# Two routed expert pairs in every unit of the shared expert, begun half a block later, and the last routed rows sent two to a product

## What is computed

```python
x = x + 0.5 * moe(layernorm(x))
x = x + mamba(layernorm(x))
x = x + 0.5 * moe(layernorm(x))

def moe(x):                              # 4096 tokens, 64 experts, 4 chosen for each token
    choice, weight = top4(x @ router_w.T + router_bias), softmax weights of those four, normed
    # each expert takes its first 64 tokens (capacity 64); the rest is dropped
    for e in experts:
        y[e] = (silu(x[tok[e]] @ gate_w[e].T) * (x[tok[e]] @ up_w[e].T)) @ down_w[e].T
        out[tok[e]] += y[e] * w[e]
    # the shared expert, hidden width 1024, sees every token
    return out + (silu(x @ sh_gate.T) * (x @ sh_up.T)) @ sh_down.T
```

## Time and profile before

| | us |
|---|---|
| median of 3 runs | 2441.6 (2437.28 to 2442.83) |
| profiled execution | 2441.09 |
| its span | 2439.3 |
| PE busy | 2349.8 (96% of the span) |
| DVE busy | 1415.3 (58%) |
| ACT busy | 956.4 (39%) |
| POOL busy | 665.4 (27%) |

### The profile page before, as it was taken

The page is one execution under the profiler, slowest core; times in us unless marked ns, Lnnn a source line. Parts: engine busy times, 40 slices in busy tenths (PEclk is TensorE's granted clock), DMA queues, the critical chain, the costliest instruction groups (busy, mean ns, idle before and its releaser), DMA issues.

```text
span 2439.3 us, 41942 instructions
## 1 busy us (share of the span) xinstructions
PE 2349.8 (96%) x16732; PEld 2073.8 (85%) x16732; DVE 1415.3 (58%) x3236; ACT 956.4 (39%) x1665; POOL 665.4 (27%) x524
## 2 busy tenths in 40 slices
PE   5999999999999999999999999998999999999995
PEld 5999997777788888888888889997999998787774
DVE  5777662222238777777777777776777762322221
ACT  4332332222236554445554555554333332323220
POOL 1244443111221222222222223220244443111121
PEclk9999999999998999999999999999999999999997
DMA  7644224877754110111111111013253314877758
GB/s 244 206 147 153 79 72 152 249 230 238 244 146 130 35 27 27 27 27 27 27 27 27 37 34 27 19 52 133 103 185 130 104 55 148 240 228 232 223 142 172
DMA packets 102754, 292.82 MB, mean 120 GB/s; under 512 B 22498, under 2 KB 22754, under 8 KB 91872
## 3 DMA queue, kind: packets, MB, share of 16 engines
q1 hardware_dynamic: 55216, 198.87, 23.3%
q0 software_dynamic: 47344, 91.27, 16.4%
HBM read 197.28 MB, written 151.80 MB: 143 GB/s over the span
## 4 chain that ended last, share of the span: by engine, by line
PE 93%; DVE 2%; DMA 1%; issue 1%; ACT 1%; another core or an unknown queue 0%; DVEq 0%; SPq 0%; POOLq 0%; ACTq 0%
PE m_p_ab L1559 5%; PE m_p_ab L1561 5%; PE m_p_ab L1560 5%; PE m_p_x L1559 3%; PE m_p_x L1561 3%; PE m_p_x L1560 3%; PE p_gate_b L688 3%; PE p_gate_a L688 3%; PE p_up_a L688 3%; PE p_up_b L688 3%; PE m_p_y L1660 3%; PE p_out_b L688 3%; PE p_gate_b L690 2%; PE p_gate_b L689 2%; PE p_x_a L786 2%; PE p_up_a L690 2%
## 5 line engine op out<-in xcount | busy, mean ns | idle before, releaser
L1852 DVE SCALAR_TENSOR_TENSOR m_xt<-m_ssm,m_convw,m_xt 128x256 f32<-128x256 f32 x384 | 218.9, 583 | 57.5 <-ACT m_ssm L1428 48.3
L1559 PE MATMUL m_p_ab<-m_ht_hi,m_wi_b_hi 128*128 128x256 f32 x640 | 182.4, 285 | 2.5 <-ACT m_gate L1400 2.5
L1561 PE MATMUL m_p_ab<-m_ht_hi,m_wi_b_lo 128*128 128x256 f32 x640 | 180.0, 281 | 0.0
L1560 PE MATMUL m_p_ab<-m_ht_lo,m_wi_b_hi 128*128 128x256 f32 x640 | 179.9, 281 | 0.0
L437 POOL DMA_INDIRECT slot_rows<-a_hr,a_slot_now x128 | 130.8, 1022 | 142.1 <-PE p_gate_a L690 85.7
L437 POOL DMA_INDIRECT slot_rows<-b_hr,b_slot_now x128 | 130.3, 1018 | 141.3 <-PE p_gate_b L690 85.6
L688 PE MATMUL p_gate_a<-a_hts_hi,a_w_hi 128*128 128x256 f32 x512 | 148.8, 291 | 7.3 <-DVE a_hts_lo L968 7.2
L688 PE MATMUL p_gate_b<-b_hts_hi,b_w_hi 128*128 128x256 f32 x512 | 148.4, 290 | 5.2 <-issue 5.1
L688 PE MATMUL p_up_a<-a_hts_hi,a_w_hi 128*128 128x256 f32 x512 | 148.9, 291 | 0.0
L688 PE MATMUL p_up_b<-b_hts_hi,b_w_hi 128*128 128x256 f32 x512 | 148.1, 289 | 0.0
L690 PE MATMUL p_gate_a<-a_hts_hi,a_w_lo 128*128 128x256 f32 x512 | 146.3, 286 | 0.0
(11 more groups left out here) (352 smaller groups left out, 7467.0 us busy)
## 6 DMA issues: line engine op xcount, KB each, us to landing
a_ew<-in_ew SPq DMA_DIRECT2D x32, 1536.0 KB, 7.2
b_ew<-in_ew SPq DMA_DIRECT2D x32, 1536.0 KB, 7.4
after_ffn<-a_zeros POOLq DMA_DIRECT2D x6, 2048.0 KB
out<-b_zeros POOLq DMA_DIRECT2D x6, 2048.0 KB
slot_rows<-a_zeros POOLq DMA_DIRECT2D x1, 8336.0 KB, 41.9
a_rows<-slot_rows SPq DMA_DIRECT2D x32, 260.5 KB, 8.5
b_rows<-slot_rows SPq DMA_DIRECT2D x32, 260.5 KB, 8.4
a_xr<-in_x SPq DMA_DIRECT2D x8, 1024.0 KB
```

Source lines behind the costliest of these rows:

```text
L1559: t.matmul(out, l_hi, r_hi_, start=first, stop=False)
L1560: t.matmul(out, l_hi, r_lo_, start=False, stop=False)
L1561: return t.matmul(out, l_lo, r_hi_, start=False, stop=last)
L1852: ins_ = v.scalar_tensor_tensor(xt[:, m, :], ssm[:, m, i:i + BM], convw[:, m, i:i + 1], xt[:, m, :], ALU.mult, ALU.add)
```

## The change

Three things change together. (1) Pairs no longer take two positions each but one and a half: gate and up of the even pair stand at p = 0 of a unit and those of the odd pair at p = 2. The first is at g = 117, the last down product at g = 165. The odd pair's `turn_prod` moves into the middle of the next unit's gate product. (2) The last 512 tokens' rows go out two to a product, over the second half of block 8 and the first half of block 9. (3) SP issues the first three pairs' loads in block 9 at g = 12*b + 6, and at that position a pair's loads now stand ahead of `load_xs`.

```diff
-PAIR_AT = (NR + 1) * POS + 3
+PAIR_UNIT = (NR + 1) * UN + 3
@@ positions of the pairs
         def begins(g):
-            q, odd = divmod(g - PAIR_AT, 2)
-            return q if not odd and 0 <= q <= PAIRS else None
-        def turns(g):
-            q, odd = divmod(g - PAIR_AT, 2)
-            return q if odd and 0 <= q < PAIRS else None
+            u, p = divmod(g, 3)
+            q = 2 * (u - PAIR_UNIT) + (p == 2)
+            return q if p != 1 and 0 <= q <= PAIRS else None
+        def turns_rows(g):
+            u, p = divmod(g, 3)
+            q = 2 * (u - PAIR_UNIT) + p
+            return q if p > 0 and 0 <= q < PAIRS else None
+        def turns_product(g):
+            u, p = divmod(g, 3)
+            q = 2 * (u - PAIR_UNIT) + (0 if p == 1 else -1)
+            return q if p < 2 and 0 <= q < PAIRS else None
@@ sync
-                        if g == b * POS + 6 and b + 2 < NS:
-                            load_xs(b + 2)
-                        if g == b * POS + POS - 1 and b == NR:
-                            for q in range(EU):
-                                load_pair(q)
                         q = begins(g)
                         if q and q - 1 + EU < PAIRS:
                             load_pair(q - 1 + EU)
+                        if g == b * POS + 6 and b + 2 < NS:
+                            load_xs(b + 2)
+                        if g == b * POS + 6 and b == NR + 1:
+                            for q in range(EU):
+                                load_pair(q)
@@ gpsimd
-                for b in range(NR + 1):
+                inv_std(1)
+                for b in range(1, NR + 2):
...
-                            if u >= UN // 2 and 1 <= b:
+                            if u >= UN // 2 and b <= NR:
                                 pool.wait_ge(full, b * UN + u + 1)
-                                some = 4 if b == NR else 2
-                                send_rows(b - 1, some * (n - UN), some)
+                                send_rows(b - 1, 2 * (n - UN), 2)
@@ tensor, gate_or_up, between the two halves m of a gate product
+                    if g == 0 and m == 1 and turns_product(3 * i) is not None:
+                        turn_prod(turns_product(3 * i))
@@ tensor, experts_at
-            if g == PAIR_AT - 1:
-                turn_rows(0)
                 q = begins(g)
                 if q is not None and q < PAIRS:
                     expert_gate_up(q)
                 if q:
                     expert_down(q - 1)
-                q = turns(g)
-                if q is not None:
-                    turn_prod(q)
-                    if q + 1 < PAIRS:
-                        turn_rows(q + 1)
+                q = turns_product(g)
+                if q is not None and g % 3:
+                    turn_prod(q)
+                q = turns_rows(g)
+                if q is not None:
+                    turn_rows(q)
```

More of the change, by code:

```diff
@@ L487, in program @@
                                 send_rows(b - 2, TR * K // 2 + 2 * n, 2)
-                            if u >= UN // 2 and 1 <= b:
+                            if u >= UN // 2 and b <= NR:
                                 pool.wait_ge(full, b * UN + u + 1)
-                                some = 4 if b == NR else 2
-                                send_rows(b - 1, some * (n - UN), some)
+                                send_rows(b - 1, 2 * (n - UN), 2)
                         if u == UN // 2 - 1 and b + 1 < NR:
                             inv_std(b + 1)
-                    if 1 <= b <= CLEARS:
+                    if b <= CLEARS:
                         clear_acc(b - 1)
@@ L612, in experts_at @@
             def experts_at(g):
-                if g == PAIR_AT - 1:
-                    rows_out(0)
                 q = begins(g)
@@ L619, in experts_at @@
                     expert_out(q - 1)
-                q = turns(g)
-                if q is not None and q + 1 < PAIRS:
-                    rows_out(q + 1)
+                q = turns_rows(g)
+                if q is not None:
+                    rows_out(q)
             def early(step):
@@ L1012, in experts_at @@
             def experts_at(g):
-                if g == PAIR_AT - 1:
+                if turns_rows(g) == 0:
                     dve.wait_ge(rows_loaded[0], 16)
@@ L1017, in experts_at @@
                     know(0)
+                q = turns_product(g)
+                if q is not None:
+                    product_turned(q)
                 q = begins(g)
@@ L1022, in experts_at @@
                         know(q + 1)
-                q = turns(g)
-                if q is not None:
-                    product_turned(q)
             def early(step):
```

## The result

The changed kernel takes 2399.79 us (median of 4 executions, 2398.56 to 2400.55) against 2440.17 us for the kernel before on the same chip (4, 2437.28 to 2442.83): a ratio of 0.9827, 95% interval 0.9812 to 0.9843. The forecast was 2432 with a range from 2411. The gain is 40 us in place of 9.6. The profiled execution spans 2397.7 us, 41.6 less than before's 2439.3.

The account below looks back on a forecast made before the run. PE was taken as bound, 96% busy, with losses at block 8's end, the chain of adds and the kernel's end. Layer a -6.6 and layer b -3.0 made 2441.1 - 9.6 = 2431.5, by the median 2432; range 2411 to 2461.

Parts of the forecast that it names:

- the chain: POOL's serial adds, one per pair and block; predicted to pace pairs from the fifth on and set layer b's end.
- s = 8.2: Assumed us per add, issue to issue, over the whole chain; between 5.69 without loads and 9.07 with a load beside each.
- 10.2 + 36 s - 308.4: Layer b's change: the chain starts 10.2 us later, takes 36 steps of s against 308.4 us now; forecast -3.0.
- Layer a, forecast -6.6: Layer a's sum: -8.2 for the removed wait after block 8, +1.6 for turns, 0 for PE waiting on adds.
- The stall: End of block 8: PE idle on a late semaphore, then slow clock; removal counted as -8.2 us layer a, -7.3 layer b.
- The 16 turns inside gate products, priced at +1.6: Turning the product inside the gate product adds 16 tile changes per layer, 0.1 us each: +1.6 in layer a, nothing in b.
- PE's wait for result buffers: Layer a's pairs: with five result buffers PE is free of the chain up to s = 8.3, so 0 us.
- Later start: Pairs begin six positions later, 17.5 us; PE loses nothing, but layer b's chain starts at +17.5 - 7.3 = +10.2.
- Order on SP: A pair's loads ahead of the token load cover one pair, 7.9 us, of a wait reaching 20 us; no gain counted.
- The merges begin about 10 us earlier: Kernel's end: merges start when the last pair is added, about 10 us earlier, with 51 us full DMA and 8 after.
- The rival with the nearest time, 2406: Adds become quick, s 7.0 or less, and PE bounds layer b's end: 2406 us, chance 0.12.
- the rival that they stay: The waits at the end of block 8 have another cause than the burst; 15.5 us come back: 2447 us, chance 0.13.

Follow-up runs that it names:

- Experiments 6: Kernel before, with every pair's weights load held back by one position, still evenly spaced: 2436.31 us, ratio 0.9984.
- experiment 7: Kernel before, with only every second pair's weights load held back by one position, so load distances alternate: 2425.07 us, ratio 0.9939.
- experiment 9: Kernel before, loading only the first half of each expert's packed weights from the fourth pair on: 2425.05 us, ratio 0.9936.
- experiment 8: Kernel before, with only SP's new order, a pair's loads ahead of the token load: 2440.4 us, ratio 1.0001.
- experiment 4: Changed kernel with the old order on SP, a block's token load ahead of the pair's loads: 2419.57 us, ratio 0.9928.
- experiments 2: Changed kernel without the new sends and later start (four to a product in block 8, pairs from unit 37): 2411.27 us, ratio 0.9889.
- 5: Changed kernel with the last 16 sends three to a product in block 8, two in block 9, pairs one unit earlier: 2395.37 us, ratio 0.9819.
- experiment 12: Version with last sends three to a product and pairs one unit earlier, run again beside the changed kernel: 2396.97 us, ratio 0.9817.
- experiment 3: Changed kernel with the last routed rows sent four to a product in block 8 again, all else as changed: 2421.89 us, ratio 0.9929.

## Why the prediction was wrong, step by step

**The step that failed is the time per step of the chain, s = 8.2,** in the term "10.2 + 36 s - 308.4" of layer b. It measured 7.43, and the 36 steps took 267.4 us in place of 295.2, 27.8 less. 7.43 lies between its bounds (5.69 and 9.07). The error has two parts.

The larger one needs no experiment. The prediction knew that a step without a load takes 5.69 us, but spread its 8.2, "nearer to the loaded end", over the whole chain. The last seven steps, from block 12's add to block 13's, have no weights load beside them and took 41.1 us where 8.2 gives 57.4: 16.3 of the 27.8 us. SP had asked for the last weights at 2287.13.

The rest is the loaded step: 212.3 us for 27 steps where 8.2 gives 221.4, 9.1 us, and 2.4 us in the first two. The prediction took it for a price of the add beside its load. Experiments 6, 7 and 9 showed in its place that the 9.07 of the kernel before was no such price: the chain had fallen in step with the loads, 9.15 us apart, and steps of 8.2 and 7.96 came out when only the loads' distances or bytes changed. In the changed kernel the stretch looked at had loads 7.65 us apart and steps of 7.67, and the mean from block 9 to 12, with the blocks' adds in it, is 7.86. How much of this its uneven distances do stays open. That loads would be asked for some 6.5 and 9.1 us apart was right (6.30 and 9.15).

**Layer a, forecast -6.6, measured -10.2** (the last finish 744.11, before 754.35). The stall is -8.1 of it (block 8's finish 391.57 against 400.70, less 1.0 that is there from the first block on and that the change does not explain). The 16 turns inside gate products, priced at +1.6, cost nothing that can be seen: from block 8's finish to the last it is 1.1 us less than before. PE's wait for result buffers was 0, as said; ACT waited 1.9 us for them, in two places.

**Layer b's start.** Later start less the stall less layer a: forecast 10.2 - 6.6 = +3.6, measured 2069.78 - 2069.09 = +0.7, as layer a gave more.

**Order on SP, "no gain of its own".** True in the kernel before (experiment 8), wrong in the packed one: some 20 us (experiment 4). The prediction looked at it as cover for one pair's 7.9 us and missed that without that cover PE itself stops.

**The end.** "The merges begin about 10 us earlier" should have read 40. That they end the kernel, that the DMA engines are full for 51 us and 8 follow, and that PE's last product is not what ends it, was right. The rival with the nearest time, 2406, had the adds quick and PE bounding the end; experiments 2, 5 and 12 end so, 5 us behind PE, and the changed kernel, 11 us behind it, does not. The sum with the measured terms: -10.2 in layer a; 17.5 - 7.1 = +10.4 for start and stall of layer b, and +0.5 for the chain's start against that; 267.4 - 308.4 = -41.0; -1.3 behind the chain; together -41.6.

**The stalls.** Both are gone, and the burst is their cause (experiment 3); the rival that they stay is out. The Trainium skill's price for an add, an estimate of 2.6 us by the page "DMA: Bandwidth & Descriptors", section on the anatomy of one DMA on the gpsimd path, is again not borne out: the shortest landing between 2180 and 2300 us is 4.9 us in the changed kernel, and 4.8 in experiments 6 and 7. The same page says, in its section on queues, rings and completion order, that a DMA engine takes turns between the queues that have work, a packet at a time. The trace agrees only so far that such an add is not served first: the one issued at 2217.54 landed 8.1 us later, 1.7 us behind the load issued at 2216.98, which took 7.0, and adds get longer with the load's bytes (median 5.6 us beside 0.75 MB, 8.1 beside 1.5 MB). Whether packets of the two alternate these landings do not show.

## What to carry to other kernels

A serial chain of transfers that runs beside evenly spaced loads can lock to their distance, and then looks like a fixed price per transfer: before using such a price, compare it with the distance of the loads, and look whether one load starts in every step. Loads in uneven turn at the same mean distance (experiment 7) or smaller ones (experiment 9) freed it here; with denser loads the steps got shorter with the loads' distance. Price a chain in stretches, those with loads beside them and those without: one mean step for all of it was the larger part of the miss here. An order of requests on one queue that costs nothing at one spacing can stop the bound engine at a denser one, so the order belongs to the packing and is to be priced with it. And where a chain and an engine end nearly together, move the start of the chain last: one unit earlier, with the last sends three to a product, was worth 6 us here.

## What the runs showed of the hardware

- The adds became shorter while the DMA engines became busier: from 2110 to 2300 us the share went from 0.79 to 0.91 and the rate from 238 to 274 GB/s, and the median landing from 8.1 to 6.8 us. Busier DMA engines need not mean longer transfers.
- When a load starts matters as much as that it runs: in layer b's first five adds, a 1.5 MB load issued 1.4 to 1.6 us ahead of an add made it land in 7.5 us (median, kernel before), one issued 1.5 to 1.7 us behind it left it at 5.1 (experiment 6), and a 0.75 MB load 1.4 to 1.6 us ahead gave 5.4 (experiment 9). An add without loads took 4.8.
- Twelve indirect sends issued without a break hold back a semaphore of PE for DVE and POOL by some 6 us (experiment 3, in both layers). Six without a break, in experiment 12, do not: DVE's product starts at 380.08 there. What in the chip holds it back stays open, and between six and twelve nothing was tried.
